# Four graph layers on one core: the first layer's outputs completed group by group, and six places for raw tiles

## The reference, cut to what matters

```python
h = max(layernorm(x), 0)
x = x + (adj / rowsum(adj)) @ h @ W_in + (adj.T / colsum(adj)) @ h @ W_out       # layer 0
h = max(layernorm(x), 0)
x = x + swish(adj @ swish(adj @ h @ W1 + b1) @ W1 + b1)                            # layer 1, adj used twice
h = max(layernorm(x), 0);  x = x + relu(norm(adj + I) @ h @ W2 + b2)               # layer 2
h = max(layernorm(x), 0);  x = x + relu(norm(adj + I) @ (h @ W3) + b3)             # layer 3
```

## Time and profile before

| | us |
|---|---|
| median of 3 runs | 1153.92 (1153.37 to 1154.3) |
| the profiled execution, its own time | 1153.61 |
| its span | 1151.8 |
| PE busy | 1120.3 (97%) |
| DVE busy | 1046.6 (91%) |
| ACT busy | 909.1 (79%) |
| DMA | 408.36 MB, 355 GB/s on average |

### The profile page before, as it was taken

The page is one execution under the profiler, slowest core; times in us unless marked ns, Lnnn a source line. Parts: engine busy times, 40 slices in busy tenths (PEclk is TensorE's granted clock), DMA queues, the critical chain, the costliest instruction groups (busy, mean ns, idle before and its releaser), DMA issues.

```text
span 1151.8 us, 14790 instructions
## 1 busy us (share of the span) xinstructions
PE 1120.3 (97%) x5120; PEld 919.1 (80%) x5120; DVE 1046.6 (91%) x1419; ACT 909.1 (79%) x1265; POOL 48.0 (4%) x40
## 2 busy tenths in 40 slices
PE   4999999999999899999999999999999999999997
PEld 3778888888876678888888887888888888888886
DVE  5999989989899999987988999999999999998985
ACT  6888897887777868787887787888777788776772
POOL 0000000000000000000000211201112111000000
PEclk9999999999999999999999999999999999999999
DMA  9999999999988889999999999999999999998984
GB/s 348 339 337 394 391 410 377 352 407 381 341 301 304 300 282 400 401 381 362 396 346 381 312 383 332 369 379 340 376 340 358 379 327 376 353 394 331 401 330 171
DMA packets 113546, 408.36 MB, mean 355 GB/s; under 512 B 12608, under 2 KB 13632, under 8 KB 113472
## 3 DMA queue, kind: packets, MB, share of 16 engines
q1 hardware_dynamic: 113472, 407.42, 95.1%
HBM read 405.27 MB, written 2.10 MB: 354 GB/s over the span
## 4 chain that ended last, share of the span: by engine, by line
PE 83%; DVE 10%; ACT 4%; issue 2%; DMA 0%; ACTq 0%; DVEq 0%
PE bank L604 52%; PE bank L608 27%; DVE a_lo L385 6%; PE bank L615 3%; ACT a_hi L270 3%; PE bank L636 1%; ACT act_raw L294 1%; DVE x_sb L482 1%; DVE h_lo L408 1%; DVE zt L390 1%; DVE stats L415 0%; ACT a_hi L268 0%; DMA x_sb<-in_x_dram 0%; DVE zt L394 0%; DVE mv L419 0%
## 5 line engine op out<-in xcount | busy, mean ns | idle before, releaser
L385 DVE TENSOR_TENSOR a_lo<-raw,a_hi 128x1024 fp32r<-128x1024 f32 x768 | 898.3, 1219 | 64.7 <-ACT a_hi L268 49.9
L268 ACT ACTIVATE a_hi<-raw 128x1024 fp32r<-128x1024 f32 x512 | 520.6, 1054 | 81.1 <-DMA raw<-in_adj_t_dram 65.5
L604 PE MATMUL bank<-a_hi,h_hi 128*128 128x512 f32 x1536 | 480.0, 394 | 14.6 <-ACT a_hi L270 14.5
L608 PE MATMUL bank<-a_lo,h_hi 128*128 128x512 f32 x1536 | 479.1, 393 | 9.3 <-DVE a_lo L385 7.7
L604 PE MATMUL bank<-a_hi,h_lo 128*128 128x512 f32 x1536 | 474.6, 390 | 0.0
L608 PEld LDWEIGHTS bank<-a_lo,h_hi 128*128 128x128 f32 x1536 | 285.0, 188 | 85.8 <-DVE a_lo L385 28.6
L604 PEld LDWEIGHTS bank<-a_hi,h_hi 128*128 128x128 f32 x1536 | 284.2, 188 | 72.7 <-DVE h_lo L408 14.5
L604 PEld LDWEIGHTS bank<-a_hi,h_lo 128*128 128x128 f32 x1536 | 288.9, 188 | 61.4
L270 ACT ACTIVATE a_hi<-raw 128x1024 fp32r<-128x1024 f32 x256 | 269.7, 1055 | 29.4 <-DMA raw<-in_adj_dram 8.5
L303 ACT ACTIVATE act_raw<-x_sb,lnbias,lnscale 128x128 f32<-128x128 f32 x96 | 39.7, 484 | 47.0 <-DVE lnbias L443 47.0
L252 POOL TENSOR_TENSOR std<-mv,eps_sb 128x4 f32<-128x4 f32 x16 | 17.4, 1088 | 931.6 <-DVE mv L419 931.6
(11 more groups left out here) (50 smaller groups left out, 183.4 us busy)
## 6 DMA issues: line engine op xcount, KB each, us to landing
raw<-in_adj_t_dram SPq DMA_DIRECT2D x640, 512.0 KB, 6.5
raw<-in_adj_dram SPq DMA_DIRECT2D x128, 512.0 KB, 6.3
x_sb<-in_x_dram SPq DMA_DIRECT2D x4, 512.0 KB, 10.5
out_dram<-x_sb SPq DMA_DIRECT2D x8, 256.0 KB, 7.0
w_sb<-in_L_gnn_W_dram SPq DMA_DIRECT2D x3, 64.0 KB, 11.3
b_sb<-in_L_gnn_b_dram SPq DMA_DIRECT2D x3, 64.0 KB, 8.1
w_sb<-in_L_gnn_W_in_dram SPq DMA_DIRECT2D x1, 64.0 KB, 12.3
w_sb<-in_L_gnn_W_out_dram SPq DMA_DIRECT2D x1, 64.0 KB, 12.3
```

Of the source, the lines that this page charges most:

```text
L268: act.activation(sub(a_hi, n), sub_raw(n), ACT.Copy).then_inc(sub_hi, 1)
L385: dve.tensor_tensor(sub(a_lo, n), sub_raw(n), sub(a_hi, n).bitcast(F32), ALU.subtract).then_inc(sub_lo, 1)
L604: pe.matmul(bank[half][:, :], weights, hi_a[:, half * GW:(half + 1) * GW], start=start and weights is hi_w, stop=False)
L608: last = pe.matmul(bank[half][:, :], hi_w, lo_a[:, half * GW:(half + 1) * GW], start=False, stop=stop)
```

## The change

Layer 0 is put in another order, with two kinds of run. For b = 0 to 3: first, for every later group d and for both products, a partial run of eight substeps that holds what blocks of group b contribute to outputs of group d; it is drained into `acc` (`prod_t` for group 0), copied by ACT when b = 0 (16 copies of 512 columns) and added by DVE otherwise (24 additions). Then both products of group b itself run to their end, over the groups c from b on. Group b is complete after substep 111, 191, 239 and 255 for b = 0 to 3. `acc` grows from 16 to 24 KB a partition; `raw` shrinks from eight places to six. Of x only blocks 0 to 3 are loaded ahead of tile 0; the normalization of the input is done by four blocks, the last piece at substep 80. In the sweeps the second half's work comes `LATER` = 16 substeps after the first's. The last four substeps of the whole kernel are done for the first bank and then for the second, and the last four blocks of the output leave in two pieces. The weights, the sums and the number of matmuls stay as they were.

```diff
-    RAWS = 8
+    TAIL = 4
+    RAWS = 6
...
-        acc = sb("acc", [P, NB * P])
+        acc = sb("acc", [P, 2, NG - 1, CW])
...
+        run_ps = (banks[0:2], banks[2:4], banks[4:6])
...
+        for b in range(NG):
+            for kind in range(2):
+                for d in range(b + 1, NG):
+                    runs.append((kind, d, b))
+                    seq += [(len(runs) - 1, kind, d, b * CB + i, i == 0, i == CB - 1) for i in range(CB)]
+                    run_end.append(len(seq) - 1)
+            runs += [(0, b, b), (1, b, b)]
+            for c in range(b, NG):
+                for kind in range(2):
+                    seq += [(len(runs) - 2 + kind, kind, b, c * CB + i, c == b and i == 0, c == NG - 1 and i == CB - 1)
+                            for i in range(CB)]
+            run_end += [len(seq) - 1 - CB, len(seq) - 1]
+            step_end.append(len(seq) - 1)
...
-        LATER = 8
+        LATER, LATER_FIRST = 16, 8
...
+        DRAIN = {run_end[r] + 7 - 3 * (runs[r][2] >= 2) + half: (r, half) for r in range(len(runs)) for half in range(2)}
...
+        DEGREES = {step_end[b] + (9, 9, 4, 4)[b]: b for b in range(NG)}
+        for b in range(NG):
+            for half in range(2):
+                ROW_WEIGHTS[step_end[b] + (2, 2, 2, 1)[b] + (2, 2, 1, 1)[b] * half] = (b, half)
+                ROW_ADD[step_end[b] + (11, 11, 6, 5)[b] + 2 * half] = (b, half)
+                COL_WEIGHTS[step_end[b] + (16, 16, 10, 8)[b] + (2, 2, 2, 1)[b] * half] = (b, half)
+                COL_ADD[step_end[b] + (25, 25, 13, 12)[b] + 2 * half] = (b, half)
...
+        LO = {step_end[b] + at: 2 * b + half for b, half, at in
+              ((0, 0, 41), (0, 1, 61), (1, 0, 38), (1, 1, 47), (2, 0, 23), (2, 1, 29), (3, 0, 21), (3, 1, 25))}
...
+        FIRST_STATS = {0: 1, 6: 2, 19: 3, 32: 4, 45: 5, 58: 6, 71: 7}
+        FIRST_STD = {0: 1, 10: 2, 23: 3, 36: 4, 49: 5, 62: 6, 75: 7}
+        FIRST_AFFINE = {0: 1, 11: 2, 24: 3, 37: 4, 50: 5, 63: 6, 76: 7}
+        FIRST_RELU = {1: 1, 14: 2, 27: 3, 40: 4, 53: 5, 66: 6, 79: 7}
...
             load_x(0)
-            for n in range(4):
-                load_tile(n)
+            load(0)
             load_x(1)
-            for n in range(4, RAWS):
-                load_tile(n)
-            for i in (2, 3):
-                load_x(i)
+            for n in range(1, RAWS):
+                load(n)
+            load_x(2)
...
+            for n in range(RAWS, len(substeps)):
+                load(n)
+                if n in (16, 32):
+                    load_x(2 + n // 16)
...
+            def copy_partial(r, half):
+                kind, d, _ = runs[r]
+                act.wait_ge(sub_used, run_end[r] + 1)
+                if d == 0 and kind == 1:
+                    act.wait_ge(z_ready, z_row(0, half) + 1)
+                act.activation(partial(kind, d, half), run_ps[r % 3][half][:, :], ACT.Copy).then_inc(part_copied, 1)
...
+            first_std(0)
+            for n in range(S0):
+                _, kind, d, k, _, _ = seq[n]
+                hi(n, (row_part if kind else col_part)[:, k, d:d + 1])
+                if n == 0:
+                    first_relu(0)
+                first_layer(n)
...
+            def add_partial(r, half):
+                kind, d, _ = runs[r]
+                part = partial(kind, d, half)
+                dve.wait_ge(sub_used, run_end[r] + 1)
...
+                dve.tensor_tensor(part, run_ps[r % 3][half][:, :], part, ALU.add).then_inc(part_added, 1)
...
+            for n in range(S0):
+                r, _, _, k, first, last = seq[n]
+                if first and r >= 3:
+                    copied, added = drained(r - 3)
+                    pe.wait_ge(part_copied, copied)
+                    if added:
+                        pe.wait_ge(part_added, added)
...
+                products(n, h_hi[0][:, k, :], h_lo[0][:, k, :], run_ps[r % 3], first, last)
+                first_layer(n)
...
             for half in range(2):
-                finish(SWEEPS, NG - 1, half)
+                for s in range(NS - TAIL, NS):
+                    tail_products(n_of(SWEEPS, NG - 1, s), hi_set[:, s, :], lo_set[:, s, :], bank, half, s == NS - 1)
+                    if half == 1 and s == NS - TAIL // 2 - 1:
+                        finish(SWEEPS, NG - 1, 0)
+            for quarter in range(2):
+                finish_quarter(quarter)
```

More of the change, by code:

```diff
@@ L117, in build_gnn_stack, with run_of, drained, partial @@
         out_done = sem("out_done")
-        def n_of0(u, s):
-            return u * US + s
+        runs = []
+        seq = []
+        step_end = []
+        run_end = []
+        for b in range(NG):
[11 more added lines that the diff above has]
+            step_end.append(len(seq) - 1)
+        assert len(seq) == S0
+        def run_of(kind, b):
+            return runs.index((kind, b, b))
+        def drained(r):
+            first = sum(b == 0 for _, _, b in runs[:r + 1])
+            return 2 * first, 2 * (r + 1 - first)
         def n_of(sweep, g, s):
             return S0 + ((sweep - 1) * NG + g) * NS + s
[L127 to L132, removed]
+        substeps = [(adj if kind else adj_t, d, k) for _, kind, d, k, _, _ in seq]
+        substeps += [(adj_t, g, k) for sweep in range(SWEEPS) for g in range(NG) for k in range(NB)]
         def sub_raw(n):
             return raw[:, n % RAWS, :]
+        def partial(kind, d, half):
+            return prod_t[:, half, :] if d == 0 else acc[:, kind, d - 1, half * GW:(half + 1) * GW]
         def sub(t, n):
@@ L195, in halves, with late @@
+        FIRST_AFFINE = {0: 1, 11: 2, 24: 3, 37: 4, 50: 5, 63: 6, 76: 7}
+        FIRST_RELU = {1: 1, 14: 2, 27: 3, 40: 4, 53: 5, 66: 6, 79: 7}
+        FIRST_LO = {1: 1, 15: 2, 28: 3, 41: 4, 54: 5, 67: 6, 80: 7}
         def halves(at, s):
             return [h for h in range(2) if at[h] == s]
-        def late(at, s):
-            return [h for h in range(2) if at is not None and at + h * LATER == s]
+        def late(at, g, s):
+            return [h for h in range(2) if at + h * (LATER if g else LATER_FIRST) == s]
@@ L325, in silu, with first_layer @@
                     act.activation(zt[:, :], zt[:, :], ACT.Silu).then_inc(silu_ready, 1)
[L327 to L348 removed]
+            def first_layer(n):
+                if n in FIRST_STD:
+                    first_std(FIRST_STD[n])
+                if n in FIRST_RELU:
+                    first_relu(FIRST_RELU[n])
+                if n in DRAIN and runs[DRAIN[n][0]][2] == 0:
+                    copy_partial(*DRAIN[n])
+                if n in STD:
+                    ln_std(STD[n])
+                if n in RELU:
+                    ln_relu(0, RELU[n])
+                if n == 40:
+                    act.wait_ge(ident_made, 2)
+                    act.activation(ident_r[:, :], ident[:, :], ACT.Copy).then_inc(ident_made, 1)
+                if n == DSQ[1]:
+                    act.wait_ge(dsq_ready, 1)
+                    act.activation(d_isqrt[:, :], d_isqrt[:, :], ACT.Sqrt).then_inc(dsq_ready, 1)
+            first_std(0)
+            for n in range(S0):
[4 more added lines that the diff above has]
+                first_layer(n)
             for sweep in range(1, SWEEPS + 1):
@@ L355, in _ @@
                         if ps == 0:
[L356 to L364, removed]
+                            first_layer(n_of(sweep, g, s))
                             continue
@@ L609, in products, with tail_products @@
                 last.then_inc(sub_used, 1)
+            def tail_products(n, hi_w, lo_w, bank, half, stop):
+                cols = slice(half * GW, (half + 1) * GW)
+                pe.wait_ge(sub_hi, n + 1)
+                for weights in (hi_w, lo_w):
+                    pe.matmul(bank[half][:, :], weights, sub(a_hi, n)[:, cols], start=False, stop=False)
+                pe.wait_ge(sub_lo, n + 1)
+                last = pe.matmul(bank[half][:, :], hi_w, sub(a_lo, n)[:, cols], start=False, stop=stop)
+                if stop:
+                    last.then_inc(tail_ready, 1)
             def weight_product(zi, half, src, w):
```

327 lines of the change are left out of this document (159 added, 168 removed).

## The result

The changed kernel is slower: 1217.22 us median of six runs (1206.89 to 1222.16) against 1153.85 us for the kernel before (1152.27 to 1155.84). The ratio is 1.0543, 95% interval [1.0517, 1.057]. The forecast said slower, at 1160, with 1188 as its upper end: the sign held, the size was off by a factor of ten, 63 us instead of 6, and the range did not hold the time.

The account below looks back on a forecast made before the run. PE, 97% busy with 1102.6 us of its own work, was taken as the bound, leaving 49 us to win. Terms -4.1 + 1.8 + 0 - 1.9 + 12.8 - 2.8 = +5.8 gave about 1160; range 1131 to 1188, the forecast's own 1152 to 1172.

Parts of the forecast that it names:

- Start: Before and at the first matmul: at about 10.4 us, -4.1; 2.7 given back by substep 4, starting at 18.5.
- End: After the last matmul: one half's chain runs under the last matmuls, -2.8 us (-1.5 to -3.2).
- Six places: Raw tile loop: loads land in 5.4 us (3.5 to 6.2), hardly any slack; sweeps lose +12.8 us more than before.
- the walk through a group of sweep 3: 32 substeps followed with 5.4 us landing: DVE ends at 49.1, PE needs 47.2, 1.9 lost; 5.7 loses about 4.
- Groups without normalization: Sweep 1 and the last three groups of sweep 4: need 43 to 45 us each, nothing lost.
- Layer 0: Substeps 4 to 80 +1.8 us, 80 to 112 as before, 112 to 280 -1.9 us.
- With the loop of six I take 12.5: Substeps 112 to 280, groups completed one by one: 12.5 us lost instead of 14.4, -1.9 (-7.2 to +9).
- the forecast's floor: Substeps 112 to 280: DVE needs 251.5 us against PE's 244.3, so 7.2 lost instead of 14.4 even with better spread.
- B: Rival for the whole kernel: six places are enough, only work counts, -21.8 us, 1132; chance 0.27.
- C: Rival for the raw loop: landing takes 5.0 us with so few in flight, -8.1 us, 1146; chance 0.15.
- D: Rival for the raw loop: landing takes 5.7 us or more, +31.4 us, 1185; chance 0.15.
- The signs named ahead: Trace signs of the loop: first 64 substeps over 95 us, DMA waits in sweeps, landing 5.2 to 5.6 us.

Follow-up runs that it names:

- e2: The kernel after with eight raw places instead of six and rings of seven instead of eight: 1140.15 us, ratio 0.9882 to the kernel before.
- e1: The kernel before with six raw places instead of eight, nothing else changed: 1200.60 us, ratio 1.0397 to the kernel before.

## Why the prediction was right about the sign and wrong about the size

**Start: right on the first matmul, short by a microsecond behind it.** First matmul forecast at 10.4 us, seen at 10.39. The lines of ACT at the start of the kernel after, beside the earlier trace rows:

```profile
6.26 1.06 ACT L317 ACTIVATE a_hi<-raw 128x1024 fp32r<-128x1024 f32 x1 [1.03 <-DMA raw<-in_adj_t_dram]
...
11.57 0.30 ACT L322 ACTIVATE zt<-zt,eps_sb 128x4 f32<-128x4 f32 x1 [1.96 <-DVE zt L444]
```

The second shows the piece that gives time back: ACT waits until 11.57 for the statistics of blocks 4 to 7, as forecast. Substep 4 then starts at 19.39, where the forecast had 18.5. Tile 6 was issued at 11.60, not at about 15. Its place had been free since 8.67, and its landing was not the normal one on which the forecast had hidden the delay: it took 8.96 us, to 20.56. ACT, done with tile 5 at 19.18, stood 1.4 us for it. The chain of waits of the kernel after has this load as one of its longest pieces:

```profile
11.60 8.96 DMA raw<-in_adj_t_dram
```

**End: right within its range.** Forecast -2.8. The lines of DVE at the end, beside the earlier trace rows:

```profile
1210.53 0.61 DVE L634 SCALAR_TENSOR_TENSOR zt<-bank,d_isqrt,b_sb 128x128 f32<-128x128 f32 x2 [0.71 <-PE bank L703]
1211.17 0.42 DVE L639 SCALAR_TENSOR_TENSOR x_sb<-zt,x_sb 128x256 f32<-128x256 f32 x1
```

From the last matmul of a tile to the span's end it is 5.4 us instead of 8.5, with one more weight product before that mark (0.9), so -2.2 net.

**Six places: right mechanism, wrong number.** The step that failed is "With few in flight queueing shrinks, so I take 5.4 us to land". It was 6.1 [after's loads above]. The forecast had two points, 3.1 in flight landing in 5.5 us and 4.6 in 6.2, and took its number from below the first. The first comes from a stretch in which DVE was late: a landed tile stayed in its place for 8.8 us on average, and few loads were in flight for that reason. (Its 5.5 is also the median of 32 loads only; the other 16 of that stretch landed in 4.9.) Six places had not 3.1 in flight but 4.0, and a straight line between the forecast's own two points gives 5.9 there. In the probe the loads at a steady four take 5.7 us, and what counts is that this means 1.45 us or more a tile.

How much this explains: the walk through a group of sweep 3, with 6.1 in place of 5.4 and nothing else changed, gives 51.9 us instead of 49.1. Measured are 202.1 / 4 = 50.5, where PE needs 47.2: 3.3 lost a group instead of 1.9. The walk is steep, 4 us a group for each microsecond of landing. So 5.7 us gives about 50.3 in it, 3 lost a group, and the "about 4" that the prediction has for 5.7 does not come out of its own walk.

**Groups without normalization: wrong.** The forecast was nothing lost. Sweep 1 took 143.3 us for three groups, 7.5 more than before, and sweep 4 6.8 more. With 6.1 us the bare turn is 8.4 us, 1.40 a tile, and with the copies, the swish and the split a tile of sweep 1 stayed 2.7 us after landing instead of 2.3, which makes 8.8 us, 1.47 a tile, over PE's 1.416: the slack the forecast saw there (43 to 45 us against 45.3) was not there. Sweeps together: +39.0 measured, 0.9 of that the moved product, against +12.8.

**Layer 0: wrong, and here the step is another one.** Substeps 0 to 64 were forecast slightly slower (+1.8 to substep 80), measured +6.1; 64 to 112 were forecast as before, measured +4.4, and the two weight products of before are no longer in them, so 6.2; 112 to 288 forecast -1.9, measured 287.1 - 266.5 = +20.6 with two more products in it, 18.8 net. For the last of these the prediction walked nothing through: "With the loop of six I take 12.5" is a number without a sum behind it. What it had no number for is the time that a tile stays in its place after landing. The prediction has 2.32 us for it "if no engine is doing something else". From the landing of each tile to the end of its `a_lo` it was 3.0 us on average in the sweeps and 3.6 in layer 0, where landing itself took 5.9. DVE's extra work and ACT's root, relu and copies are more in layer 0, and the sum for the degrees, which ACT finishes behind each tile, puts 0.12 us at the least between ACT's end and DVE's start, where it is 0.03 in the sweeps. A turn of 5.9 + 3.6 = 9.5 us makes 1.59 us a tile; I had put a loop of 1.36 to 1.42 there and little more. The gain that the rest was to bring is real, seen in e2: 112 to 288 take 262.9 instead of 266.5 with two more products, 5.4 net (the forecast's floor said 7.2), 0 to 64 1.7 less instead of some 6.

**The rivals.** B, that six places are enough, put the whole at 1132; without the loop it is 1140. C needed a landing of 5.0 us and did not come. D, 5.7 us or more, is the one whose condition came true, at a chance of 0.15, and its price of +31.4 is half of the 63. It had 10 us for layer 0, where 31.1 were lost, and 28.3 for the sweeps, where it was 38.1 without the moved product. It put nothing on groups without normalization.

**The signs named ahead.** 64 substeps in over 95 us were to speak for the loop: 103.1. ACT was to wait for the DMA in most substeps of sweeps 2 and 3: it did, 179 times in 256. Waits for `a_lo` or `a_hi` there were to be some 15 us: PE's weight loads stood 22.8. In layer 0's second part waits for `a_lo` were to be around 10 us instead of 16: in 184.9 to 472.0, where the kernel before has 16.1, they were 30.2, so this sign failed, and with it the term for that part. "I am wrong if the time to landing falls with the places": it fell only from a median of 6.4 to 6.1.

**Why the order after lost 77 us to six places and the order before only 47.** By the profiled executions, layer 0 lost 38.2 us in the new order (after against e2) and 13.5 in the old (e1 against before), the sweeps 39.7 and 27.8. So with six places the new order of layer 0 is the slower one, 461.7 us against e1's 444.1, and with eight the faster, 423.5 against 430.6. The turn of a place in layer 0 is 5.90 + 3.64 us in the kernel after and 5.82 + 3.39 in e1 (landing, then the time to the end of `a_lo`): most of the difference is that ACT and DVE keep the tiles longer in the new order. That the old order also hides more of it, where DVE holds PE back anyway, is a reading of the stretches; no run was made for it. In the sweeps the tiles are kept equally long, 3.01 us in both, and the whole difference is in landing, 6.13 us against 6.01, or 0.02 us a tile and some 10 us for all. Why is open: `LATER` accounts for 2.6 at most, and e1 ran on the chip on which the probe's loads were also the quicker ones (1.45 to 1.48 us a tile with four in flight against 1.55). No run has both kernels with six places on one chip.

## What to carry to other kernels

Before giving up buffers, count loads in flight: places minus the hold time over the pace. Take the hold time with all the other work of the engines in it, since here it was 3.0 to 3.6 us and not the bare 2.3. Then ask what rate the DMA gives at that count; a short probe of nothing but loads tells it. Where the pace that the kernel needs lies between two counts, its time has a step there: at 1.42 to 1.47 us for a tile of 512 KB, four in flight were too few and five enough. When an outer loop of load, prepare and free sets the pace, the wait of the busiest engine is not where time is to be won (12.5 us of it could go without a gain), and SBUF for the ring behind the loop is better spent on the places ahead of it: a ring of seven or six cost nothing here, six places 47 us and more.

## What the runs showed of the hardware

- Loads of 512 KB (128 x 4 KB): 134, 212, 265, 362, 407 and 405 GB/s with 1, 2, 3, 4, 5 and 6 in flight, with nothing beside them but copies of eight columns on DVE. One alone lands in 3.7 us, two in 4.8, three and four in 5.7, five in 6.2. A second probe on another chip had 1.55 us a tile with four, where this one has 1.45 to 1.48.
- With three and with four tiles in flight the rate is the same whether a tile is one DMA or two of 512 columns (2.0 and 2.0 us, 1.55 and 1.52), so it follows the bytes in flight and not the number of DMAs; two DMAs of 64 partitions each are slower than one of 128 (2.2 us a tile with 3, 4 or 5 places, against 1.3 to 2.0). Why four whole loads don't fill the DMA was not settled: its busy share in the stage of four is 0.98 at 362 GB/s, and 1.03 at 407 with five, so the share alone does not tell a filled DMA from one that is short of loads.
